# Norm factors spread over 32-row tiles, sums of squares in eights, new engine orders

## The reference

```
def l2norm(t):
    return t / jnp.maximum(jnp.linalg.norm(t, axis=-1, keepdims=True), 1e-12)

def attn_layer(x, Wqkv, qs, ksc, Wo):
    q, k, v = split heads of x @ Wqkv          # 16 heads of 64
    q = l2norm(q) * qs
    k = l2norm(k) * ksc
    q = q * cos * scale + rotate_half(q) * sin * scale
    k = k * cos / scale + rotate_half(k) * sin / scale
    out = local_attention(q, k, v)             # windows of 32, each sees itself and the one before
    return out @ Wo

for i in range(6):
    x = attn_layer(shift_tokens(x), ...) + x
    x = ffn_layer(shift_tokens(x), ...) + x
```

## Time and profile before

| | us |
|---|---|
| median of 3 runs | 2266.87 (2265.04 to 2267.53) |
| the profiled execution's own time | 2274.98 |
| its span, first to last instruction | 2273.2 |
| mean granted clock of TensorE | 0.962 |

### The profile page before, as it was taken

The page is one execution under the profiler, slowest core; times in us unless marked ns, Lnnn a source line. Parts: engine busy times, 40 slices in busy tenths (PEclk is TensorE's granted clock), DMA queues, the critical chain, the costliest instruction groups (busy, mean ns, idle before and its releaser), DMA issues.

```text
span 2273.2 us, 84305 instructions
## 1 busy us (share of the span) xinstructions
PE 2019.9 (89%) x35280; PEld 1310.9 (58%) x35280; DVE 1615.8 (71%) x3316; ACT 1093.3 (48%) x1911; POOL 891.1 (39%) x1166
## 2 busy tenths in 40 slices
PE   6989896789998999979999799999799998899996
PEld 2333332466665666656666566766566765666664
DVE  5556645678876788866878677878687876777872
ACT  2333332355554555544555455646355654455553
POOL 0000001445544545443545353545354544444540
PEclk9999998899998999989999999999999998999996
DMA  1000100545555655454656455556465545555550
GB/s 58 5 9 5 51 0 11 82 80 81 83 88 100 93 82 84 78 101 84 95 82 89 98 85 81 91 84 87 86 104 79 91 82 94 89 89 81 83 87 25
DMA packets 72441, 168.15 MB, mean 74 GB/s; under 512 B 16496, under 2 KB 23408, under 8 KB 71408
## 3 DMA queue, kind: packets, MB, share of 16 engines
q0 software_dynamic: 36864, 100.71, 33.1%
q1 hardware_dynamic: 35456, 65.55, 11.1%
HBM read 20.45 MB, written 1.05 MB: 9 GB/s over the span
## 4 chain that ended last, share of the span: by engine, by line
PE 61%; DVE 15%; DMA 11%; issue 9%; POOL 2%; ACT 1%; SPq 1%; DVEq 0%; POOLq 0%; ACTq 0%
PE ps L922 13%; DMA big<-big 9%; PE ps L955 8%; PE ps L844 6%; PE ps L933 4%; PE ps L1009 4%; PE ps L992 4%; PE ps L979 3%; DVE big L743 3%; DVE big L740 3%; PE ps L1029 3%; PE ps L1022 3%; PE ps L1065 2%; POOL big L425 2%; PE ps L865 2%
## 5 line engine op out<-in xcount | busy, mean ns | idle before, releaser
L425 POOL DMA_DIRECT2D big<-big x768 | 607.5, 1494 | 93.7 <-DVE big L743 80.3
L922 PE MATMUL ps<-big,wn_sb 128*128 128x256 f32 x1536 | 404.7, 401 | 42.1 <-DMA wn_sb<-in_wn 22.2
L493 ACT ACTIVATE big<-ps 128x512 f32<-128x512 f32 x384 | 228.2, 597 | 399.7 <-PE ps L922 393.5
L922 PEld LDWEIGHTS ps<-big,wn_sb 128*128 128x128 f32 x1536 | 280.4, 195 | 119.8 <-issue 35.5
L751 DVE TENSOR_TENSOR big<-big,ps 128x512 f32<-128x512 f32 x384 | 243.7, 681 | 122.5 <-PE ps L945 81.9
L740 DVE TENSOR_TENSOR big<-ps,tab 128x512 f32<-128x512 f32 x384 | 258.5, 682 | 46.8 <-ACT big L493 46.8
L506 ACT ACTIVATE big<-ps 128x512 f32<-128x512 f32 x192 | 114.7, 597 | 358.9 <-PE ps L955 358.9
L756 DVE TENSOR_REDUCE top<-ps 128x8 f32<-128x512 f32 x192 | 123.3, 684 | 223.6 <-PE ps L979 223.6
L416 POOL TENSOR_TENSOR big<-big 128x512 f32<-128x512 f32 x96 | 121.8, 1269 | 357.8 <-ACT big L510 357.8
L743 DVE TENSOR_TENSOR big<-ps,tab 128x512 f32<-128x512 f32 x384 | 257.7, 681 | 0.0
L1065 PE MATMUL ps<-big,wo_sb 128*128 128x256 f32 x768 | 217.1, 386 | 1.9 <-issue 1.9
(11 more groups left out here) (146 smaller groups left out, 3119.9 us busy)
## 6 DMA issues: line engine op xcount, KB each, us to landing
big<-big POOLq DMA_DIRECT2D x768, 128.0 KB, 4.8
big<-big SPq DMA_DIRECT2D x96, 256.0 KB, 3.7
big<-big SPq DMA_DIRECT2D x96, 192.0 KB, 3.9
wn_sb<-in_wn SPq DMA_DIRECT2D x6, 1536.0 KB, 7.6
wo_sb<-in_wo SPq DMA_DIRECT2D x6, 512.0 KB, 5.2
w_sb<-in_w SPq DMA_DIRECT2D x6, 341.0 KB, 3.9
w_sb<-in_w SPq DMA_DIRECT2D x6, 192.0 KB, 4.9
big<-in_x SPq DMA_DIRECT2D x8, 128.0 KB, 2.2
```

What stands on the lines that cost most here:

```text
L425: eng.dma_start(rot[to:to + 32, at:at + 4, :], src[32 * r:32 * r + 32], accum_op=ALU.add).then_inc(added[i], 16)
L493: eng.activation(sq[:, two, :], ps[:, i % 2, :].rearrange("p (a t) -> p a t", a=2), ACT.Square).then_inc(sq_d, 1)
L922: mm = eng.matmul(ps[:, k % 2, a * T:a * T + T], wn_sb[:, u * P:u * P + P], sT, start=True, stop=True)
```

## The change

Three things change together.

Sums of squares: g1 and g3 take the place of g0 to g3. Each issues eight matmuls, first those of four even places, then those of four odd ones, and adds to `sums` twice. The maps `QUAD` and `SLOT` say in which block of 32 rows and in which row of it a unit's sum lies, so that the two units of a pair share a block. s4 to s7 wait for the first eight (`sums` at 2).

Spread: R0, R2, R4 and R6 take the place of R0 to R7. A step serves the two pairs n and n+1, whose sums lie in different blocks of 32 rows; each matmul takes only the 32 rows of its block as contraction, and the matmuls of the two pairs alternate, one into bank 0 and one into bank 1. The step waits until both H of the step before have read their banks, and an instruction that adds to the new semaphore `r_go` stands ahead of its matmuls. H(n) still waits for its own pair.

Orders: `PE_PLAN`, `ACT_PLAN` and `DVE_PLAN` are new; `POOL_PLAN` stays.

```diff
--- before.py
+++ after.py
@@ -41,6 +41,11 @@
 BIG = 32 * 1024
 
 
+QUAD = [u // 2 % 2 + 2 * (u // PAIRS) for u in range(UNITS)]
+SLOT = [u % 2 + 2 * (u // 4 % 2) for u in range(UNITS)]
 def shape_constants():
 
     f = np.float32
@@ -78,7 +83,7 @@
     rsel = np.zeros((P, UNITS, P), f)
     for u in range(UNITS):
         for c in range(3):
-            rsel[32 * (u % 4) + 8 * c + 2 * (u // 4) + p // D, u, p] = 256
+            rsel[32 * QUAD[u] + 8 * c + 2 * SLOT[u] + p // D, u, p] = 256
     parts = -np.stack([(m // 8 >= 1) & (m < 24), m // 8 == 2], 1).astype(f)
     xones = np.zeros((P, 4, 32), f)
     for j in range(4):
@@ -235,7 +240,7 @@
         sc_d, max_d, sub_d, ex_d, den_d, rinv_d, pt_d, ptev, ov_d, on_d, ot_d, oev, wo_d, x_d, w_go, s_go, vf_free, y2_d, den_h, den_s = (
             sem(n) for n in ("sc_d", "max_d", "sub_d", "ex_d", "den_d", "rinv_d", "pt_d", "ptev", "ov_d", "on_d", "ot_d", "oev",
                              "wo_d", "x_d", "w_go", "s_go", "vf_free", "y2_d", "den_h", "den_s"))
-        chain, nchain, nmid = sem("chain"), sem("nchain"), sem("nmid")
+        chain, nchain, nmid, r_go = sem("chain"), sem("nchain"), sem("nmid"), sem("r_go")
 
         nmean, nxc, nsq, nvar, nva, nln, ny, nxn, nt = (
             sem(n) for n in ("nmean", "nxc", "nsq", "nvar", "nva", "nln", "ny", "nxn", "nt"))
@@ -267,13 +272,13 @@
 
 
         PE_PLAN = [(x_[0], int(x_[1:])) for x_ in """
-            S0 k0 k1 F1 S1 k2 k3 T0 g0 T1 F2 k4 k5 W0 W1 g1 g2 k6 T2 k7 U0 T3 g3 W2 W3 U1 F4 O0 O1 O2 U2 O3 U3
-            F5 R0 R1 O4 R2 O5 R3 O6 R4 F6 R5 R6 O7 F7 R7 V0 V1 V2 V3""".split()]
+            S0 k0 F1 k1 F2 S1 k2 k3 T0 T1 g1 k4 k5 W0 W1 T2 k6 k7 T3 U0 g3 W2 F4 U1 O0 W3 O1 F5 R0 O2 O3 U2 U3
+            R2 F6 O4 R4 O5 O6 O7 R6 F7 V0 V1 V2 V3""".split()]
         ACT_PLAN = [(x_[0], int(x_[1:])) for x_ in """
-            s0 s1 x0 F1 s2 s3 t0 F2 t1 s4 s5 x1 s6 t2 s7 u0 t3 F3 n0 u1 F4 u2 u3 F5 v0 v1 v2 v3""".split()]
+            s0 F1 s1 x0 s2 s3 F2 t0 t1 s4 x1 s5 t2 s6 s7 t3 F3 u0 n0 F4 u1 F5 u2 u3 v0 v1 v2 v3""".split()]
         DVE_PLAN = [(x_[0], int(x_[1:])) for x_ in """
-            X0 X1 D0 D1 c0 c1 d0 d1 X2 X3 D2 c2 d2 c3 d3 D3 Z0 f0 c4 d4 c5 d5 f1 Y0 f2 c6 f3 Z1 n0 d6 c7 Y1 N1
-            d7 N2 N3 N4 N5 N6 H0 H1 H2 F5 H3 H4 F6 H5 H6 H7 F7 e0""".split()]
+            X0 X1 D0 D1 c0 c1 d0 d1 X2 X3 D2 c2 D3 d2 c3 d3 Z0 f0 c4 f1 d4 c5 d5 Y0 f2 c6 f3 c7 n0 Z1 d6 d7 N1
+            N2 N3 N4 N5 N6 Y1 H0 H1 F5 H2 H3 F6 H4 H5 H6 H7 e0 F7""".split()]
         POOL_PLAN = [(x_[0], int(x_[1:])) for x_ in """
             A0 F0 Z0 m0 Z1 m1 m2 m3""".split()]
 
@@ -489,7 +494,7 @@
                         two = slice(2 * (i % 4), 2 * (i % 4) + 2)
                         eng.wait_ge(proj, it * PAIRS + (i + 1))
                         if i >= 4:
-                            eng.wait_ge(sums, it * 4 + (i // 2 - 1))
+                            eng.wait_ge(sums, it * 4 + 2)
                         eng.activation(sq[:, two, :], ps[:, i % 2, :].rearrange("p (a t) -> p a t", a=2), ACT.Square).then_inc(sq_d, 1)
                     if kind == "n":
 
@@ -923,27 +928,35 @@
                     mm.then_inc(proj, 1)
 
                 def head_sums(g):
                     eng.wait_ge(sq_d, it * PAIRS + (2 * g + 2))
-                    if g == 0 and Bh:
+                    if g == 1 and Bh:
                         eng.wait_ge(ss_d, it)
                         eng.wait_ge(x_d, it - 1 + FREE)
-                    for n in range(4 * g, 4 * g + 4):
-                        u = ORDER[n]
-                        q = u % 4
-                        mm = eng.matmul(ps[32 * q:32 * q + 32, 2, 0:T], sumsel[:, u // 4, :], sq[:, n % 8, :],
-                                        start=g == 0, stop=g == 3, skip_group_check=True)
-                    mm.then_inc(sums, 1)
+                    for a in range(2):
+                        for n in range(4 * g - 4 + a, 4 * g + 4, 2):
+                            u = ORDER[n]
+                            q = QUAD[u]
+                            mm = eng.matmul(ps[32 * q:32 * q + 32, 2, 0:T], sumsel[:, SLOT[u], :], sq[:, n % 8, :],
+                                            start=g == 1 and a == 0, stop=g == 3 and a == 1, skip_group_check=True)
+                        mm.then_inc(sums, 1)
 
                 def spread(n):
                     if n == 0:
                         eng.wait_ge(r_d, it + 1)
-                    if n < 2:
-                        eng.wait_ge(rot_d, it * PAIRS + (7 + n))
+                        eng.wait_ge(rot_d, it * PAIRS + 8)
                     else:
-                        eng.wait_ge(hat_d, it * PAIRS + (n - 1))
+                        eng.wait_ge(hat_d, it * PAIRS + n)
+                    eng.sem_inc(r_go, 1)
                     for a in range(2):
-                        mm = eng.matmul(ps[:, n % 2, a * T:a * T + T], rselb[:, 2 * HATS[n] + a, :], n_parts, start=True, stop=True)
-                    mm.then_inc(rb, 1)
+                        for m in (n, n + 1):
+                            u = 2 * HATS[m] + a
+                            q = QUAD[u]
+                            mm = eng.matmul(ps[:, m % 2, a * T:a * T + T], rselb[32 * q:32 * q + 32, u, :], n_parts[32 * q:32 * q + 32, :],
+                                            start=True, stop=True, skip_group_check=True)
+                            if a == 1:
+                                mm.then_inc(rb, 1)
 
                 def values(j):
                     if j < 2:
```

## The result

The changed kernel is slower: 2277.18 us median (2271.11 to 2290.07, 19 runs) against 2270.40 (2260.95 to 2282.06, 19 runs) on the same chips, a ratio of 1.0034 with a 95% interval of 1.0019 to 1.0049. I had forecast 2265 on 2266.87, that is 0.9992. The change is small, but clear of the noise, and it went the other way from the one I leant to.

A forecast was written before the change was run, and what follows sets the result against it. PE is nearly always occupied, but the steady round ends through m3's landing, H5, R7, V0. Steady rounds 35.65 against 35.72, 27 x -0.07 = -2, the 20 long ones 0: 2266.87 becomes 2265; range 2240 to 2288.

The forecast's parts named there:

- The likeliest case: Round's end: m3 issued 1.44 earlier, given back in the order R6, F7; steady round 35.65, total 2265, chance 0.36.
- the front: Start of the round up to the end of g3: g3 ends at 21.94 against 22.09, worth 0.15.
- with 4.88 to land, H5 starts at 33.1: Landing of m3: 4.88 after its last issue at 28.25, so H5 starts at 33.1 (32.75 to 33.25).
- rival D: POOL transfers without a gap: the last lands 0.5 later, H5 at 33.6, V0 at 36.15; 2283, chance 0.17.
- The prediction's own sign: PE stalls on issue over the run: a change of more than 5 us in sum would show the prediction wrong.
- The 20 long rounds: Intervals with stalls, weights or layer joins: transfer already hidden behind the stall; change 0, bounds -0.2 and +0.25 each.
- C: Spread: row tiles not side by side or weights not loaded ahead; R 0.64, +21, 2288, chance 0.14.
- B: Round's end: the transfer no longer ends it and latencies are short; V0 at 34.9, about 2241, chance 0.33.
- The price of R: Spread on PE: each new R costs 0.42, of it 0.21 for form changes; four cost 1.70 against 1.76.
- a full drain: Form changes around R: draining TensorE fully at 0.17 each way would make a step 0.55; 0.42 was taken.
- My claim on r_go: Semaphore step ahead of each R: 0 beyond the switch, bounds 0 and 0.05 x 4.

The follow-up runs named there:

- e9: The changed kernel with m3 also waiting for N3, which puts a gap ahead of m3 on POOL; ratio to the kernel before 1.0106.
- e4: The changed kernel with the last four pairs reordered so that H5 needs only m2, and H6 and H7 need m3; ratio to the kernel before 0.975.
- e5: The kernel before with the last pairs reordered so that H5 no longer needs m3 and H6 does; ratio to the kernel before 0.994.
- e11: e4 with the spread's matmuls over all 128 rows in place of 32-row tiles; ratio to the kernel before 0.9789.
- e7: e6 with each of the eight spread steps in 32-row tiles, still one pair and one bank a step; ratio to the kernel before 1.0067.
- e1: The changed kernel with F7 ahead of R6 in TensorE's order, nothing else; ratio to the kernel before 0.990.
- e2: The new orders alone, with the old steps for sums of squares and spread, against the kernel before; ratio 0.9922.
- e6: The kernel before with sums of squares in two steps of eight and the spread unchanged; ratio to the kernel before 0.9978.

## Why the prediction was wrong

The likeliest case was that m3 is issued 1.44 earlier and that the 1.44 are given back in the order R6, F7, with V0 at 35.65. The mechanism held. POOL's train ends at 28.35 (predicted 28.25), DVE is ready for H5 at 32.3 (32.75), H5 is released by the transfer, R6 and F7 stand behind it, and V0 comes 2.65 after H5 (2.55). Of the front, g in 1.00 and k4 waiting for d2 held too.

The step that failed is "with 4.88 to land, H5 starts at 33.1". I took the landing to be the same with and without a gap ahead of m3. It is not: 4.66 with the gap, 5.11 without, so 0.45 of the 1.44 is lost before H5 can start; I had that only as rival D, with a chance of 0.17. The 4.88 was one round's value and not the mean of 4.66, which covered half of this by accident: with the mean I would have been further off. The last issue also ends 0.10 later than I had it. H5 comes at 33.45, 0.35 later than predicted, and with the 0.10 of the tail the round is 35.65 + 0.45 = 36.10; measured 36.12. e9 shows that the gap sets the landing, e4 and e5 that the transfer ends the round.

A second term was missing. The sum has nothing for the clock, read at 1.00 in both rounds of the earlier trace rows, and the new order leaves a wait of 1 us and more ahead of R6, where R7 had 0.39. Five of the 27 rounds run partly at the lower clock and grew by 1.44 each, not 0.38. The prediction's own sign, stalls on issue changing by more than 5, did appear: they changed by 16.5. But they fell, which hides a part of the loss. The 20 long rounds, taken at 0, grew by 0.11 each without their stalls, within their bounds, though I read them wrongly: in four of them H5 had waited over 2 us for the transfer already before. Four of the five at the layers' ends now have H5 waiting for the transfer, by 0.3 to 0.6, where none had.

Rival D's place and its point of decision (H5 later than 33.2) were right, and its +16 us is near the 17.9 by which the rounds grew apart from stalls; the timed kernels differ by only 0.34% (7.7 us). C did not happen: e11 and e4 differ by 0.09, and R takes as long for four matmuls in two row blocks as for two in one (e7). B came about only when the transfer was taken off the path (e4, 34.89 against B's 34.9).

The price of R was too low: 0.52 at R0 where I had 0.42. What I took from the cross phase as 0.21 for both changes of form is 0.29 in e7 and 0.31 at R0, where 0.21 of the 0.52 are the stream. The Trainium skill (TensorEngine Tiling (Array Packing), Key Properties) says that a change of tiling mode drains TensorE, with no price. With my estimate from the rows of 0.17 each way for a full drain, the step would take 0.55, which is nearer than my 0.42. The Trainium skill (TensorE: Matmul & The Clock Gate, The mechanism) says that weight loads overlap running matmuls only when the row group differs. The trace does not agree, as the four matmuls of e11's R, all on the same 128 rows with other weights, take 0.43, or 0.11 each. That rule would have given C's 0.64. My claim on r_go (nothing beyond the switch) was short by 0.09 at R6.

Open is by how much the timed kernels differ for each of these reasons. In the profiled executions +17.9 less 16.5 leaves 1.4, under 0.1%. Stalls on issue sum over the whole span to 66 to 70 in all traces with the new orders and to 70 to 85 with the old. Whether an execution without the profiler has the same stalls, and falls to the lower clock in the same rounds, no run here shows. Over the timed executions the mean granted clock is 0.957 for the changed kernel and 0.956 to 0.958 for the kernel before beside the experiments, where the two profiled ones have 0.956 and 0.962.

## What to carry to other kernels

When a transfer's landing ends the round, order the work so that what needs the last transfer comes last: one edit of a list was worth 2.8% in the changed kernel and 0.6% in the old. Put independent work ahead of a step that waits for a transfer, not behind it: TensorE's idle time there costs itself, and in these traces falls of the clock came with it. When you hold a new sum against a mean, take the mean of every term and not one round's value, and ask what issuing transfers back to back does to the last of them.

## What the runs showed of the hardware

- Twelve transfers of 128 KB, issued by POOL in 9.50 us without a gap, had the last one usable 5.05 to 5.11 us after its issue on average (changed, e1, e2); with a mean gap of 0.6 to 0.8 us ahead of the last four it was 4.57 to 4.66 (before, e6, e9).
- A paired R in 32-row tiles takes 0.33 from its start to the next step's, against 0.43 for the same four matmuls over all rows (e11), and as much as two matmuls in one row block (e7), so the pairs do overlap. The step ahead of it grows by 0.09 and the one behind it by 0.10, and all together come to 0.52.
- A step of two matmuls in 32-row tiles between whole-array steps costs 0.29 more than one without tiles (e7).
- In the changed kernel's rounds without a stall TensorE's granted clock fell five times to the lower level, for 3.4 us, each time 0.7 to 1.9 us after it had restarted from 1.4 to 4.2 us of idleness. Rounds without a stall below the full clock: before 0 of 30, changed 8 of 34, e9 13 of 35, e1 1 of 34, e4 and e11 0 of 35.
